# Second expert stage: the down bias moves from TensorE and ScalarE to VectorE

## The reference

```python
logits = x @ gate_w.T + gate_b
top_vals, top_idx = jax.lax.top_k(logits, 2)
routing = softmax(top_vals)
for e in range(8):
    h = x @ w1[e].T + b1[e]
    x_glu, x_lin = h[:, 0::2], h[:, 1::2]
    y = x_glu * sigmoid(1.702 * x_glu) * (x_lin + 1.0)
    ye = y @ w2[e].T + b2[e]
    we = sum(routing * (top_idx == e))
    out = out + ye * we[:, None]
```

## Time and profile before

| what | us |
|---|---|
| median of 3 timed runs | 883.8 (882.58 to 890.34) |
| the profiled execution | 888.84 |
| its span, first to last instruction | 887.1 |
| router phase of f1 | 654 to 700 |
| expert phase of f1 | 722 to 842 |
| gather phase of f1 | 842 to 887 |
| mean granted TensorE clock | 0.87 of full |

### The profile page before, as it was taken

One profiled execution on the slowest core, in us unless ns is written; L12 is line 12 of the kernel. 1 busy time (PEld: TensorE's weight loads), 2 busy tenths in 40 slices (PEclk: granted clock), 3 DMA queues, 4 the chain that ended last, 5 costly groups with the idle time before them and its releaser, 6 DMA issues. The chain is left out here.

```text
span 887.1 us, 14166 instructions
## 1 busy us (share of the span) xinstructions
PE 653.7 (74%) x4297; PEld 542.5 (61%) x4297; DVE 540.4 (61%) x1124; ACT 349.5 (39%) x772; POOL 284.8 (32%) x264
## 2 busy tenths in 40 slices
PE   0388999865991899999990989999627139999700
PEld 0256666534881688888880778888517127888600
DVE  3138878862767355544540498998747557888533
ACT  0148778742430233333332545554206114455300
POOL 3243422201000334434322365464220033332075
PEclk9979999996995799999996889999765559999855
DMA  3000000004520311111114200000037313332144
GB/s 99 24 1 1 2 2 2 2 1 142 186 87 0 90 55 60 48 61 54 55 37 133 69 1 1 0 2 0 1 96 247 133 40 91 97 106 86 48 142 142
DMA packets 38451, 54.24 MB, mean 61 GB/s; under 512 B 7236, under 2 KB 30406, under 8 KB 38246
## 3 DMA queue, kind: packets, MB, share of 16 engines
q1 hardware_dynamic: 31608, 34.80, 12.1%
q0 software_dynamic: 6768, 18.49, 7.1%
HBM read 37.28 MB, written 15.99 MB: 60 GB/s over the span
## 5 line engine op out<-in xcount | busy, mean ns | idle before, releaser
L1532 PE MATMUL banks<-r_xt,r_w_mixed 128*128 128x256 f32 x384 | 89.7, 395 | 1.4 <-ACT r_xt L1600 1.4
L1532 PEld LDWEIGHTS banks<-r_xt,r_w_mixed 128*128 128x128 f32 x384 | 75.5, 198 | 13.3 <-ACT r_xt L1600 2.1
L1278 DVE SCALAR_TENSOR_TENSOR f0x_s<-f0x_th,banks 128x512 f32<-128x512 f32 x35 | 24.1, 688 | 82.8 <-ACT f0x_th L1237 80.3
L614 POOL TENSOR_TENSOR a_rr<-a_ms_eps,neg_half 128x32 f32<-128x32 f32 x8 | 44.0, 5504 | 88.5 <-DVE a_ms_eps L507 88.5
L1140 POOL DMA_INDIRECT f_y<-f0x_yout,f_slot_of x35 | 34.4, 984 | 101.7 <-ACT f0x_yout L1256 99.5
L1126 POOL DMA_INDIRECT f1x_xg<-f_xn,f_token_of x39 | 37.0, 949 | 75.5 <-PE banks L1177 51.0
L534 DVE TENSOR_REDUCE a_ssum<-a_e 128x6 f32<-128x1536 f32 x32 | 55.8, 1742 | 2.3 <-ACT a_e L466 2.3
L1193 PE MATMUL banks<-f_w_hi,f0x_xt_hi 128*128 x140 | 56.0, 400 | 0.2 <-issue 0.2
L1193 PE MATMUL banks<-f_w_hi,f0x_xt_lo 128*128 x140 | 55.6, 397 | 0.0
L1193 PE MATMUL banks<-f_w_lo,f0x_xt_hi 128*128 x140 | 55.3, 395 | 0.0
L1237 ACT ACTIVATE f0x_th<-banks 128x512 f32<-128x512 f32 x35 | 20.9, 597 | 86.4 <-PE banks L1193 86.4
(11 more groups left out here) (332 smaller groups left out, 1861.3 us busy)
## 6 DMA issues: line engine op xcount, KB each, us to landing
f_y<-f1x_yout SPq DMA_DIRECT2D x39, 128.0 KB
f0r_stage<-in_f_w13T SPq DMA_DIRECT2D x4, 1024.0 KB
r_y<-f_y SPq DMA_DIRECT2D x16, 256.0 KB, 6.2
f1r_stage<-in_f_w13T SPq DMA_DIRECT2D x8, 512.0 KB
x_res<-in_L_attn_x SPq DMA_DIRECT2D x2, 1024.0 KB
f0r_stage<-in_f_w2T SPq DMA_DIRECT2D x4, 512.0 KB
f_xn<-f0r_xn SPq DMA_DIRECT2D x8, 256.0 KB
f1r_stage<-in_f_w2T SPq DMA_DIRECT2D x8, 256.0 KB
```

The source lines that it names most:

```text
L614: pool.tensor_tensor(rr[:], ms_eps[:], m.neg_half[:, 0:S * NH], ALU.pow).then_inc(rr_found, 1)
L1532: last = pe.matmul(bank(1 + kind)[:, eb * T:(eb + 1) * T], r.w_mixed[:, kind, j // KB, j % KB, eb * P:(eb + 1) * P], xt[:, b % 2, j % KB, ...
```

## The change

In the f1 mixture the bias product on TensorE (L1211) and ScalarE's copy of the result (L1256) go. VectorE takes the result out of PSUM itself and adds the expert's row of b2 in the same instruction. For that `k.b2` holds b2 in plain float32 on all 128 partitions, loaded by a second DMA of 1 MB behind that of `k.b1` at the end of the router phase. GpSimd's zeroing of `k.b2`, the small copy of b2 and VectorE's two instructions that split it, at the head of the router phase, go too.

```diff
@@ router_phase
-    if v.lin_bias:
-        bias_stage2 = sb("bias2", [2, E, D])
...
-    small = 16 * (1 + 2 * bool(v.lin_bias))
+    small = 16 * (1 + bool(v.lin_bias))
     @block.sync
...
-            sp.dma_start(bias_stage2[:], A["b2"].rearrange("(o e) n -> o e n", o=1).broadcast_to([2, E, D])).then_inc(small_here, 16)
...
             sp.dma_start(k.b1[:], A["b1"].rearrange("(o e) n -> o e n", o=1).broadcast_to([P, E, 2 * v.hidden])).then_inc(b1_here, 16)
-            sp.wait_ge(b1_here, 16)
+            sp.dma_start(k.b2[:], A["b2"].rearrange("(o e) n -> o e n", o=1).broadcast_to([P, E, D])).then_inc(b1_here, 16)
+            sp.wait_ge(b1_here, 32)
     @block.gpsimd
...
-        if v.lin_bias:
-            pool.memset(f32(k.b2[:]), 0.0).then_inc(bias_zero, 1)
     @block.vector
...
         dve.wait_ge(small_here, small)
-        if v.lin_bias:
-            flat = lambda t: t[0:2].rearrange("p e n -> p (e n)")
-            dve.wait_ge(bias_zero, 1)
-            dve.tensor_copy(k.b2[0:2], bias_stage2[:]).then_inc(bias_done, 1)
-            dve.wait_ge(bias_done, 1)
-            dve.scalar_tensor_tensor(out=flat(k.b2), in0=f32(flat(k.b2)), scalar=m.neg_row[0:2, 0:1], in1=flat(bias_stage2),
-                                     op0=ALU.mult, op1=ALU.add).then_inc(bias_done, 1)
         schedule(dve, Dve())
@@ expert_phase, PE, down(t)
-                if v.lin_bias:
-                    pe.matmul(y_psum, m.ones_r[:], k.b2[:, e, :], start=True, stop=False)
...
-                                     start=(i == 0 and not v.lin_bias), stop=(i == len(steps) - 1))
+                                     start=(i == 0), stop=(i == len(steps) - 1))
@@ expert_phase, ACT, down(t)
+                if v.lin_bias:
+                    return
@@ expert_phase, DVE, up(t)
                     e = bass.ds(dve.value_load(k.expert_of[0:1, t:t + 1], min_val=0, max_val=v.experts - 1), 1)
+                    self.expert[t] = e
@@ expert_phase, DVE, down(t)
+                if v.lin_bias:
+                    dve.wait_ge(down_done, t + 1)
+                    if t >= YB:
+                        dve.wait_ge(stored[t % YB], 16 * (t // YB))
+                    dve.tensor_tensor(yout[:, t % YB, :], y_psum, k.b2[:, self.expert.pop(t), :].rearrange("p e n -> p (e n)"),
+                                      ALU.add).then_inc(y_done, 1)
```

More of the change, by code:

```diff
@@ L658, in mixture_memory @@
     if v.lin_bias:
-        k.b1, k.b2 = sb("b1", [P, v.experts, 2 * v.hidden]), sb("b2", [P, v.experts, D], F32R)
+        k.b1, k.b2 = sb("b1", [P, v.experts, 2 * v.hidden]), sb("b2", [P, v.experts, D])
     k.xn_dram = nc.dram_tensor(f"{v.tag}_xn", [TOK + 1, D], F32).ap()
@@ L703, in router_phase @@
         up_done = lg_in_psum
-    bias_zero, spare_zero, spare_stored, b1_here = (sem(n) for n in ("bias_zero", "spare_zero", "spare_stored", "b1_here"))
+    spare_zero, spare_stored, b1_here = (sem(n) for n in ("spare_zero", "spare_stored", "b1_here"))
     spare = sb("spare", [1, D])
@@ L1266, in _ @@
         class Dve:
+            expert = {}
             def pick(self, t): pass
```

## The result

| | before | after |
|---|---|---|
| median of 4 runs on the same chip | 883.26 (882.58 to 890.34) | 891.93 (891.78 to 895.44) |
| ratio, 95% interval | | 1.0078 (1.0042 to 1.0114) |
| profiled execution, span | 888.84, 887.1 | 891.78, 890.0 |
| f1 router, first instruction to first of rank | 45.62 | 46.17 |
| f1 rank, to the first `hb1` | 30.02 | 29.98 |

The changed kernel is slower: by 0.8%, or 6.9 us, by the ratio, and by 8.7 us between the medians. The forecast was 887.4, the range 881.5 to 893.5: the time lies in the range, the likeliest value is 4.5 us too low. The phases tell which term: from the third to the last `hb1` it takes 6.8 us longer instead of 3.6, while router, rank, the first two tiles and the tail together moved by less than 0.1 us (+0.55, -0.04, -0.32, -0.27).

The account below looks back on a forecast made before the run. PE bounds the expert phase before (2.66 us per tile, VectorE 2.60), VectorE's sequencer after (2.77). Expert phase +3.6 and router 0.0 on the median 883.8 give 887.4 us, range 881.5 to 893.5.

Parts of the forecast that it names:

- What bounds the phase: Expert phase: PE at 2.66 us per tile before, DVE alone 2.60; afterwards DVE's sequencer, with PE waiting for the addition.
- I take 1.69 + 1.08 = 2.77.: Expert phase, VectorE: 1.69 us from `hb1` to `h`, 1.08 to the next `hb1`; phase 3.6 us longer.
- two more instructions stand ahead of the register load: VectorE's sequencer behind `h`: 0.16 to 0.17 us more ahead of the load, so `hb1` comes 1.08 behind `h`, not 0.91.
- PE's loop through `y_done`: 2.73: Expert phase: PE's down waits for the previous tile's addition; 5.45 us per two rounds, hidden behind 2.77 by 0.04.
- Removed from PE, 0.12 per tile; ACT's copy, nothing: Expert phase: without the bias product PE's period falls from 2.66 to 2.54 us; removing ACT's 0.38 copy gains nothing.
- Overlap of VectorE's instructions: Expert phase, VectorE's engine: instructions start 0.34 us apart, allowing `hb1` 1.02 behind `h`, or 1.10 if it waits.
- Router phase, -2.6 and +2.6: f1 router: 2.6 us gained through the head, 2.6 lost to the added 1 MB load at the end; net 0.0.
- Tail: End of the expert phase: one bias product less on PE and DVE's slightly later addition balance, 0 us.
- The load falls behind the addition: Slower rival, VectorE's sequencer: register load waits for the addition; 2.94 us per tile, +9.4, 893.2; chance 0.17 with longer PE loop.
- The addition for nothing: Faster rival, expert phase: DVE absorbs the addition, period 2.60 us, with the head's gain 880.2 in all; chance 0.10.
- Router pays alone: Rival, router phase: the head's gain is lost and 2.6 us at the end remain, 890.0; chance 0.10.
- The granted clock: Rival, PE in the expert phase: clock falls as PE gets short waits, some 0.2 to 0.4 us per tile; chance 0.01.

Follow-up runs that it names:

- the kernel without bias: The changed kernel with the down bias left out (no addition, no product) and ScalarE copying y as before: ratio 0.9969 to the kernel before, 880.79 us.
- the early load: The changed kernel with VectorE's register load of the next tile moved ahead of its wait for the tanh: ratio 1.0057 to the kernel before, 892.50 us.
- the two-bank kernel: The changed kernel with the register load one tile early, 39 output buffers and y alternating between two PSUM banks: ratio 0.9988 to the kernel before, 885.16 us.

## Why the prediction was right or wrong

- **What bounds the phase.** Right: VectorE's sequencer, behind `h`, sets the period, PE pauses, and "issue" or nothing stands before `hb1`. DVE's own period of 2.60 was measured as 2.61 in the kernel without bias.
- **"I take 1.69 + 1.08 = 2.77."** This is the term that was mis-sized. For the additions without the second wait its working is right: two instructions more ahead of the load move it from 0.10 to 0.25 behind `h`, and 1.70 + 0.25 + 0.81 = 2.76. That 2.77 is nearly what was measured there (2.75 to 2.79 in the first four periods, 2.78 in the kernel without that wait) is partly luck, since PE's loop of 2.78 is what ends last in them. The step that failed is "two more instructions stand ahead of the register load": there are three from the fifth tile on. The prediction took the addition's two waits for part of the addition; one of them is a row of its own in the sequencer. It moves the load by another 0.07 and costs 0.05 per tile, shown from both sides (2.78 without it, 2.92 with one row of waits more). Some 31 periods of 0.055 make 1.7 us.
- **The long periods.** Not foreseen: four of 0.27 to 0.35, together 1.3 us. The kernel before had two of 0.22, which I read over. With the second wait and these, 99.5 + 1.7 + 1.3 = 102.5; measured 102.72.
- **PE's loop through `y_done`: 2.73.** Too short by 0.05. The six down products take 0.81 from first start to the first up product (791.68 to 792.49), not 0.70, because the first down slot is the long one, 0.21 (791.68 to 791.89; 0.22 at 781.96 in the changed kernel) against 0.11 to 0.12 for those behind it: I had used that very slot to argue that the bias product's absence gains only 0.12, and then left it out here. The loop is 2.78: above the sequencer's 2.76 without the second wait, 0.05 below the 2.83 with it. So it wasn't hidden behind 2.77 by 0.04, as forecast, and it ate what the early load freed.
- **Removed from PE, 0.12 per tile; ACT's copy, nothing.** PE's own period of 2.54 was measured as 2.55, and the product is worth nothing beside the addition (product kept: 102.58), as forecast. ACT's copy was not tested by itself.
- **Overlap of VectorE's instructions.** Right: 0.33 to 0.34 between starts of instructions of 0.42, and the two-bank kernel reaches `hb1` 1.00 behind `h`. Three full durations of 0.42 behind `h` would make 1.69 + 1.26 = 2.95 per tile; the two-bank kernel has 2.69.
- **Router phase, -2.6 and +2.6.** Both right where they were read (2.7 and 2.6), though the first chunk came 3.2 earlier, not 3.5 to 4.0, and the rest of the phase did not quite keep its length: b1 was issued 2.1 earlier, 0.6 were lost on the way. The net 46.17 against 45.62 lies within what the eight other kernels with the changed router phase show (44.9 to 46.3, mean 45.4). The longer wait of the third chunk for the store, 3.93, is as described.
- **Tail.** 0.3 us shorter instead of 0.
- **The rivals.** "The load falls behind the addition" (2.94 per tile, 893.2) is nearest in number, but did not happen: the load starts 0.32 behind `h`, ahead of the addition; the second half of that rival, a longer loop, was real but masked. "The addition for nothing" is refuted by 5.1 us. "Router pays alone" gave 890.0 by a term that wasn't there. The granted clock stayed at 1.00 in the steady stretch; what a lower one would cost in time, no run shows.
- **Base.** The change was put on the median, 883.8; the median measured beside it was 883.26. Phases by length give 6.8 + 0.55 - 0.04 - 0.32 - 0.27 = 6.7 us, close to the ratio's 6.9. The rest to 8.7 is less than the interval of the ratio leaves open (3.7 to 10.1).

What stays open is the cause of the long periods. Counted from the first `hb1`, they are the 10th, 17th, 18th and 33rd period in the changed kernel and in the one with the product kept on PE. In both kernels with two banks, and in the one with the same VectorE program and one bank, they are the 11th, 17th, 19th, 27th and 35th. So they belong to places of the program, not to chance. In the changed kernel, idle time ahead of `hb1` is booked as "issue", and removing one instruction per tile changed their number from four to one.

The DMA records of the traces show something that goes with them: small transfers of the kind "instruction". Queue q14 began one of 8 KB at 756.4, 774.4, 778.9, 800.1 and 821.4 in the steady part of the changed kernel. Each of the four long periods (ending at 755.69, 775.74, 778.92 and 821.64) has one of them inside it or 0.7 us behind it; the one at 800.1 has none. In the kernel before, the two long periods (765.77 to 768.66 and 808.59 to 811.47) have those at 767.5 and 810.3 inside. In the kernel without the store's wait the only long period (776.51 to 779.54) has the one at 778.3 inside; those at 761.5, 784.1, 806.2 and 828.4 have none. From the kind's name I suspect the supply of instructions rather than data, but what these transfers do is not shown, nor that they are the cause: not every such transfer has a long period, and no run changed them alone.

## What to carry to other kernels

Where a small engine time stands between two instructions that are late, count the sequencer's rows as well as the engine's: every wait that gets a row of its own (0.07 and 0.10 us here), every register instruction (0.06) and every register load with its register work (0.3 + 0.19 + 0.02) between them is a term. Before taking a removed wait or load as a gain, work out the next loop to the same hundredth, with its first slot at the long value (0.21 here, 0.12 for the slots behind it). And look at what is done while an engine idles at a phase's end: here a load that was waited for at a barrier and could move past it was worth more than the arithmetic that was changed.

## What the runs showed of the hardware that was not expected

- A wait with a row of its own on VectorE's sequencer costs time though nothing holds it up: its row has the same length in every tile. One of 0.021 us with one semaphore (all 35 of them) moved the register load behind it by 0.07 us (0.25 to 0.32 behind `h`), one of 0.050 us with two semaphores (0.049 to 0.050 in all 39) by 0.10 (0.32 to 0.42).
- A register load and its register work take 0.3 + 0.19 + 0.02 us of VectorE's sequencer, in the order of its program; moved ahead of `s1`, they held `s1` up by 0.10.
- GpSimd's additions and products on two partitions stopped VectorE's instructions of two SBUF inputs on all 128: 0.29 us became 3.64 and 4.13.
- 3 MB of bias rows landed during the rank phase without lengthening it (30.07 against 30.02).
- Long periods of 0.2 to 0.36 us stand at the same places of the program in different runs and, in the three kernels named above, each has an 8 KB transfer of kind "instruction" inside it or 0.7 us behind it. Cause not shown.
